# Weights and centroids laid out by channels in a clustered 1x1 convolution, and the head of its schedule reordered

## The chip, the cores and the metric

One core of one Trainium2 chip. The metric is device time in microseconds, the median of several executions. Engines are called TensorE (PE in the profile; PEld is its weight load), VectorE (DVE), ScalarE (ACT), GpSimd (POOL) and SyncE (SP), which issues the transfers.

## What is computed

The input has 8 images of 512 channels and 32 x 48 points. Each point goes to the nearest of 40 centroids by cosine; each cluster's mean over the image pulls its points, by a weight that falls with their distance; then a 1x1 convolution and a relu follow.

```python
xn = x / jnp.maximum(jnp.linalg.norm(x, axis=1, keepdims=True), EPS)
cn = centroids / jnp.maximum(jnp.linalg.norm(centroids, axis=1, keepdims=True), EPS)
sim = jnp.einsum('bchw,nc->bnhw', xn, cn)
idx = jnp.argmax(sim, axis=1)
onehot = jax.nn.one_hot(idx, N, dtype=x.dtype)
sum_x = jnp.einsum('bhwn,bchw->bnc', onehot, x)
count = jnp.sum(onehot, axis=(1, 2))
centroids_local = sum_x / jnp.maximum(count, 1.0)[..., None]
gathered = centroids_local[jnp.arange(B)[:, None, None], idx]
delta = jnp.transpose(gathered, (0, 3, 1, 2)) - x
alpha = jnp.exp(-jnp.mean(delta * delta, axis=1, keepdims=True))
y = x + alpha * delta
out = jnp.einsum('oc,bchw->bohw', W, y) + b[None, :, None, None]
return jax.nn.relu(out)
```

## The kernel before

The work is cut into 24 units of 512 points, three to an image; unit g belongs to image g // 3, and images are counted from 0 in the code (the change's words "image 2" are the second image, units 3 to 5). Channels stand on partitions in four groups (k). X[0] and X[1] hold two images, filled by turns. Every engine runs a list of instructions written out by hand, and semaphores tie them together.

Per image: `similarities(g)` multiplies centroids cT with the points; ScalarE copies the result out (`copy_sims`); `transpose_sims` turns it so that points stand on partitions; VectorE finds the first best centroid (`best_sims`, `first_best`) and writes the one-hot `oh`. `sum_clusters` multiplies it with x, for which x must have points on partitions (XT). For image 0 and for the two units in TURNED, TensorE turns x (`transpose_x`, `turn`) into the PSUM tiles gat and main, and ScalarE or VectorE evacuates it (`keep_transposed`, `keep_turned`); for the other units VectorE does it by blocks (`transpose_half`) from a blocked load XS. From the sums come the means in three bf16 parts, G (`copy_sums`, `low_clusters`, `add_halves`, `counts`, `scale_means`, `high_means`, `rest_of_mean`, `parts_of_mean`).

Per unit: `gather` brings each point its mean, `delta` on VectorE subtracts x, `square` on ScalarE and `add_chunks` on GpSimd or VectorE make squares and add channel groups, `sum_squares` on TensorE adds over partitions, `exp` on ScalarE makes alpha in the tile al, `scale` and `y_half` give y, `high_half` rounds it to its high part YH, `low_half` keeps the rest YL. Then `convolve(g, o)` multiplies in blocks of 128 output channels with three products each (WH with YH and YL, WL with YH), and `relu` evacuates. For unit 0 the first two blocks are made by `high_passes` (all products with YH), and the products with YL follow.

The weights are loaded row by row into OUT[0], each 128 x 128 block is turned on TensorE by `transpose_weights`, and `high_weights` and `low_weights` split the result into WH and WL. The centroids are loaded as rows (craw), turned on TensorE and copied to cT by ScalarE. Rows of centroids serve for the norm too. SyncE issues the centroids first, then image 0 in 12 chunks of 256 KB, the weights, the bias, image 1, and the blocked loads.

TensorE's order in the head is: warm-up products, centroids turned, similarities and transposes of image 0, weights turned (two of four groups), cluster sums of image 0, one-hot transposes, another group of weights, `add_halves(0)`, the last group, `turn(0)`, similarities of units 3 and 4, gathers of unit 0, and so on up to `convolve(0, 3)`; then the loop over units 3 to 23 begins with `gather(3, 0)`.

Of the kernel before, what the change touches and what calls it, by code (L numbers as in the profile page):

```python
# [42 lines left out]
TURNS = ((PARTS + 1, (0,)), (PARTS + 1, (1,)), (PARTS + 1, (2, 3)), (PARTS + 2, (0, 1)), (PARTS + 2, (2, 3)))  # L43
# [55 lines left out]
def build(nc, x, cent, w, bias, out):  # L99
# [3 lines left out]
    with ctx:  # L103
# [48 lines left out]
        cstat = sb("cstat", [P, 7], F32)  # L152
        Wraw = OUT[0]
# [30 lines left out]
        cT_ps, cT_done, norm_step = sem("ct_ps"), sem("ct_done"), sem("norm_step")  # L184
        wT_ps, wh_done, wl_done = sem("wt_ps"), sem("wh_done"), sem("wl_done")
# [23 lines left out]
        def wT(k):  # L209
            return (gat[:, 0, :], gat[:, 1, :], main[:, 0, :], main[:, 1, :])[k]  # L210
# [51 lines left out]
        def _(sp):  # L262
# [25 lines left out]
            sp.dma_start(craw[0:N, :], cent).then_inc(c_in, 16)  # L288
# [109 lines left out]
        def _(dve):  # L398
# [165 lines left out]
            low_weights(0)  # L564
            low_weights(1)
            low_clusters(0)
            counts(0)
            low_weights(2)
            rest_of_mean(0)
            parts_of_mean(0)  # L570
            low_weights(3)

            delta(0, 0)
            delta(0, 1)
            transpose_half(3, 0)
# [4 lines left out]
            transpose_half(3, 1)  # L580
# [12 lines left out]
            rest_of_mean(1)  # L593
            parts_of_mean(1)
            add_chunks(2, 0)
            low_half(1, 1)
# [53 lines left out]
        def _(act):  # L650
# [14 lines left out]
            def square(g, h):  # L665
                act.wait_ge(z_done, 2 * g + h + 1)
                if g < LAG:

                    act.wait_ge(wT_ps, KC)
                    act.wait_ge(const_done, 7)  # L670
                elif h == 0:
                    wait(act, s_done, folded(g - 1))
# [85 lines left out]
            def high_means(b):  # L758
# [3 lines left out]

# [3 lines left out]
            act.wait_ge(cT_ps, 1)  # L767
            a_.activation(cT[:, :, 0:N], sumP[:, 0:KC * N].rearrange("p (k n) -> p k n", k=KC),
                          ACT.Copy).then_inc(cT_done, 1)
# [9 lines left out]
            def high_weights(k):  # L779
                act.wait_ge(wT_ps, k + 1)  # L780
# [3 lines left out]
            copy_sims(1)  # L784
            keep_transposed(0, 1)
            copy_sims(2)
# [5 lines left out]
            high_weights(1)  # L792
            copy_onehot(0)
            copy_sums(0)
            evacuate_onehot()
            high_weights(2)
            scale_means(0)
            high_means(0)
            high_weights(3)
            keep_turned(0)  # L800
            act.wait_ge(b_in, 16)
            copy_sims(3)
            copy_sims(4)
# [3 lines left out]
            keep_turned(1)  # L807
            keep_turned(2)
            keep_turned(3)
            keep_turned(4)  # L810
# [5 lines left out]
            move_sums(1)  # L816
            exp(1)
            high_half(0, 1)
# [7 lines left out]
            high_half(1, 0)  # L826
            square(2, 1)
            high_half(1, 1)
# [63 lines left out]
        def _(pe):  # L892
            t_ = nc.tensor

            def similarities(g):
# [9 lines left out]
                for k in range(KC):  # L905
# [292 lines left out]
```

## Time and profile before

| | before |
|---|---|
| time, median of 3 runs | 410.26 us (409.72 to 410.3) |
| the profiled execution | 410.88 us |
| its span | 409.1 us |
| mean granted clock of TensorE | 0.999 |
| TensorE matmuls busy | 403.9 us (99%) |
| VectorE busy | 338.9 us (83%) |
| ScalarE busy | 260.7 us (64%) |
| GpSimd busy | 262.1 us (64%) |

Times inside the profile count from the start of the span; the execution's own time is 1.8 us longer than the span. Matmuls are pipelined and the durations shown overlap, so the distance between two starts says more about a matmul's cost than its duration. Busy times are of one execution.

### The profile page before, as it was taken

What the parts mean: (1) busy time and instruction counts of PE and PEld (TensorE: products, weight loads), DVE (VectorE), ACT (ScalarE), POOL (GpSimd) and SP (SyncE); (2) the same over time, 40 slices, a digit from 0 to 9 for tenths busy, and PEclk for the clock granted to TensorE, in tenths of its full rate; (3) what the DMA queues carried; (4) which work ended last, traced back from release to release, by engine and by line L of the source; (5) the groups of instructions that cost most, each with busy time, mean ns of one, the idle gap of its engine ahead of it and who ended that gap; (6) DMA issues with size and microseconds to landing.
All of it is one profiled execution on the core that took longest, in us unless ns stands there. A gap on an engine that the chain in (4) does not pass through costs nothing.

```text
span 409.1 us, 5812 instructions
## 1 busy us (share of the span) xinstructions
PE 403.9 (99%) x2088; PEld 288.2 (70%) x2088; DVE 338.9 (83%) x415; ACT 260.7 (64%) x362; POOL 262.1 (64%) x117
## 2 busy tenths in 40 slices
PE   8999999999999999999999999999999999999997
PEld 5746376775867677775867758776777758777886
DVE  2439999888899879999799898998799897898730
ACT  6566783767665684665865576656846658676641
POOL 2003773984599676994789946996769947433420
PEclk9999999999999999999999999999999999999999
DMA  7992493988499395967979575994957240222213
GB/s 256 380 248 51 88 244 84 297 252 180 172 246 266 113 281 140 272 162 183 265 198 229 191 163 188 254 256 118 276 139 226 104 129 13 103 103 104 103 68 138
DMA packets 77918, 74.51 MB, mean 182 GB/s; under 512 B 13723, under 2 KB 52891, under 8 KB 77891
## 3 DMA queue, kind: packets, MB, share of 16 engines
q1 hardware_dynamic: 77890, 74.15, 64.7%
q8 instruction: 17, 0.28, 0.3%
q14 instruction: 11, 0.08, 0.1%
HBM read 46.22 MB, written 25.17 MB: 174 GB/s over the span
## 4 chain that ended last, share of the span: by engine, by line
PE 95%; POOL 1%; DMA 1%; ACT 1%; issue 0%; DVE 0%; SPq 0%; ACTq 0%
PE main L1023 21%; PE main L1024 21%; PE main L1025 21%; PE fa L915 11%; PE sump L960 8%; PE gat L1000 5%; PE fa L924 1%; PE al L1006 1%; DMA x<-x 1%; PE main L1084 1%; PE main L1037 1%; PE al L1011 1%; POOL o L382 1%; POOL o L385 1%; PE gat L1037 1%; PE main L1055 0%
## 5 line engine op out<-in xcount | busy, mean ns | idle before, releaser
L1023 PE MATMUL main<-yh,wh 128*128 128x512 f32 (+1 forms) x376 | 152.8, 406 | 0.0
L1024 PE MATMUL main<-yl,wh 128*128 128x512 f32 (+1 forms) x376 | 146.3, 389 | 0.0
L1025 PE MATMUL main<-yh,wl 128*128 128x512 f32 (+1 forms) x376 | 146.1, 389 | 0.0
L360 POOL TENSOR_TENSOR z<-z,x 128x1024 f32<-128x1024 f32 x41 | 97.4, 2395 | 60.5 <-DVE z L519 60.5
L367 POOL TENSOR_TENSOR yl<-z,yh 128x1024 fp32r<-128x1024 f32 x43 | 103.7, 2429 | 13.8 <-ACT yh L693 13.7
L701 ACT ACTIVATE o<-main,bcol 128x512 f32<-128x512 f32 x96 | 65.1, 680 | 46.8 <-PE main L1025 45.9
L1023 PEld LDWEIGHTS main<-yh,wh 128*128 128x128 f32 x376 | 70.7, 188 | 21.4 <-issue 4.6
L1025 PEld LDWEIGHTS main<-yh,wl 128*128 128x128 f32 x376 | 70.6, 188 | 14.9
L1024 PEld LDWEIGHTS main<-yl,wh 128*128 128x128 f32 x376 | 70.7, 188 | 13.8
L374 POOL TENSOR_TENSOR xr<-xt 128x2048 f32<-128x2048 f32 x11 | 51.5, 4684 | 19.1 <-DVE xt L411 19.1
L483 DVE TENSOR_TENSOR z<-gat,x 128x1024 f32<-128x1024 f32 x46 | 55.8, 1213 | 6.1 <-PE gat L1000 6.1
L519 DVE TENSOR_TENSOR z<-z,al 128x1024 f32<-128x1024 f32 x48 | 56.3, 1210 | 0.6 <-ACT al L688 0.5
L693 ACT ACTIVATE yh<-z 128x1024 fp32r<-128x1024 f32 x48 | 50.6, 1053 | 3.6 <-POOL z L360 1.8
L915 PE MATMUL fa<-x,c_t 128*64 128x256 f32 x384 | 47.2, 394 | 0.5 <-DMA x<-x 0.5
L411 DVE STREAM_TRANSPOSE xt<-xs 128x1024 f32<-128x1024 f32 x38 | 46.1, 1225 | 0.0
L915 PEld LDWEIGHTS fa<-x,c_t 128*64 128x64 f32 x384 | 26.5, 140 | 19.3 <-issue 5.8
L673 ACT ACTIVATE sq<-z 128x1024 f32<-128x1024 f32 x21 | 22.3, 1060 | 25.7 <-DVE z L483 25.7
L673 ACT ACTIVATE gat<-z 128x1024 f32<-128x1024 f32 x21 | 21.5, 1024 | 25.2 <-DVE z L483 25.2
L419 DVE TENSOR_TENSOR xr<-xr 128x2048 bf16<-128x2048 f32 x11 | 36.7, 3338 | 0.2
L960 PE MATMUL sump<-xt,oh 128*64 128x512 f32 (+1 forms) x148 | 31.7, 537 | 0.0
L382 POOL TENSOR_TENSOR o<-o 128x512 f32<-128x512 f32 x4 | 5.1, 1284 | 36.2 <-ACT o L673 36.2
L1000 PE MATMUL gat<-oht,g 128*128 128x512 bf16 x92 | 27.8, 384 | 0.0
(139 smaller groups left out, 402.6 us busy)
## 6 DMA issues: line engine op xcount, KB each, us to landing
out<-o SPq DMA_DIRECT2D x23, 1024.0 KB, 7.2
x<-x SPq DMA_DIRECT2D x21, 1024.0 KB, 6.6
xs<-x SPq DMA_DIRECT2D x76, 256.0 KB, 5.5
x<-x SPq DMA_DIRECT2D x12, 256.0 KB, 5.4
o<-w SPq DMA_DIRECT2D x1, 1024.0 KB, 8.4
out<-o SPq DMA_DIRECT2D x3, 256.0 KB, 2.0
out<-o SPq DMA_DIRECT2D x2, 128.0 KB, 1.7
oht<-oh SPq DMA_TRANSPOSE x7, 3.7
```

The source lines that it names most:

```text
L360: pool.tensor_tensor(z, z, X[g // PARTS % 2][:, pair(h), span(g)], ALU.add).then_inc(y_pool, 1)
L367: pool.tensor_tensor(YL[g % 2][:, pair(h), :], Z[g % 2][:, pair(h), :], YH[g % 2][:, pair(h), :].bitcast(F32), ALU.subtract).then_inc(lo_p ...
L374: pool.tensor_tensor(XR[:, g % PARTS, :, :].rearrange("p t c -> p (t c)"), xt.rearrange("p t c -> p (t c)"), halfword(xt, 1), ALU.subtract ...
L483: v_.tensor_tensor(Z[g % 2][:, pair(h), :], banks(g, h)[:, :, :], X[g // PARTS % 2][:, pair(h), span(g)], ALU.subtract).then_inc(z_done, 1)
L519: v_.tensor_tensor(z, z, al[:, :].unsqueeze(1).to_broadcast([P, 2, UNIT]), ALU.mult).then_inc(za_done, 1)
L693: a_.activation(YH[g % 2][:, pair(h), :], Z[g % 2][:, pair(h), :], ACT.Copy).then_inc(hi_done, 1)
L701: a_.activation(OUT[g % 2][:, o, cols], main[:, o % 2, cols], ACT.Relu, bias=bcol[:, o:o + 1]).then_inc(relu_done, 1)
L915: last = t_.matmul(simP[u][NPAD * h:NPAD * (h + 1), :], cT[:, k, :], toks, start=(k == 0), stop=(k == KC - 1))
L960: last = t_.matmul(sumP[NPAD * h:NPAD * (h + 1), :], onehot[:, slot(u, tile), :], x_part[:, tile * C:(tile + 1) * C], start=(opens and t = ...
L1023: t_.matmul(tile, WH[:, k, rows], YH[g % 2][:, k, cols], start=(k == 0), stop=False)
L1024: t_.matmul(tile, WH[:, k, rows], YL[g % 2][:, k, cols], start=False, stop=False)
L1025: last = t_.matmul(tile, WL[:, k, rows], YH[g % 2][:, k, cols], start=False, stop=(k == KC - 1))
```

## The change

The host hands over the weights with input channels first, and a second copy of the centroids laid out by channel (partition, group, centroid). The weights go from their tile OUT[0] straight to `high_weights` and `low_weights`; the 16 transposes of weights and the four of centroids go. ScalarE's queue issues both loads of centroids, and SyncE's queue starts with image 0. The order in the head changes: similarities of unit 0 begin with k = 0 alone and four k = 0 transposes stand behind them; `transpose_sims(0)` stands ahead of unit 1's transposes; the 32 transposes of TURNED come in four steps instead of five, the first two around `add_halves(0)`. Both gathers of unit 1 stand ahead of `sum_squares_direct(0)`, and `sum_squares_direct(1)` stands behind the first half of `high_passes`. VectorE takes the halves of `transpose_half(3)` one step earlier and `low_half(1, 1)` before `parts_of_mean(1)`. ScalarE does `high_half(0, 1)` before `exp(1)`, and `high_half(1, 1)` before `square(2, 1)`.

```diff
--- before.py
+++ after.py
@@ -40,7 +40,7 @@
 TURNED = (PARTS + 1, PARTS + 2)
-TURNS = ((PARTS + 1, (0,)), (PARTS + 1, (1,)), (PARTS + 1, (2, 3)), (PARTS + 2, (0, 1)), (PARTS + 2, (2, 3)))
+TURNS = ((PARTS + 1, (0, 1)), (PARTS + 1, (2, 3)), (PARTS + 2, (0, 1)), (PARTS + 2, (2, 3)))
@@ -96,7 +96,7 @@
-def build(nc, x, cent, w, bias, out):
+def build(nc, x, cent, cent_t, w, bias, out):
@@ -181,8 +182,8 @@
         ones_done, const_done, ident_done = sem("ones_done"), sem("const_done"), sem("ident_done")
-        cT_ps, cT_done, norm_step = sem("ct_ps"), sem("ct_done"), sem("norm_step")
-        wT_ps, wh_done, wl_done = sem("wt_ps"), sem("wh_done"), sem("wl_done")
+        cT_in, cT_done, norm_step = sem("ct_in"), sem("ct_done"), sem("norm_step")
+        wh_done, wl_done = sem("wh_done"), sem("wl_done")
         xp_done, xe_dve, xe_act = sem("xp_done"), sem("xe_dve"), sem("xe_act")
@@ -207,7 +208,7 @@
         def wT(k):
-            return (gat[:, 0, :], gat[:, 1, :], main[:, 0, :], main[:, 1, :])[k]
+            return Wraw[:, k, :]
@@ -285,7 +286,6 @@
-            sp.dma_start(craw[0:N, :], cent).then_inc(c_in, 16)
             for u in range(PARTS):
@@ -561,23 +561,21 @@
             first_best(0)
-            low_weights(0)
-            low_weights(1)
+            for k in range(KC):
+                low_weights(k)
             low_clusters(0)
             counts(0)
-            low_weights(2)
             rest_of_mean(0)
             parts_of_mean(0)
-            low_weights(3)
+            transpose_half(3, 0)
             delta(0, 0)
             delta(0, 1)
-            transpose_half(3, 0)
+            transpose_half(3, 1)
             best_sims(1)
...
             delta(1, 1)
-            transpose_half(3, 1)
             scale(0, 0)
@@ -591,9 +589,9 @@
             rest_of_mean(1)
+            low_half(1, 1)
             parts_of_mean(1)
             add_chunks(2, 0)
-            low_half(1, 1)
             add_chunks(2, 1)
@@ -666,7 +664,7 @@
-                    act.wait_ge(wT_ps, KC)
+                    act.wait_ge(wl_done, KC)
                     act.wait_ge(const_done, 7)
@@ -760,13 +758,12 @@
+            act.dma_start(cT[:, :, 0:N], cent_t).then_inc(cT_in, 16)
+            act.dma_start(craw[0:N, :], cent).then_inc(c_in, 16)
...
             act.wait_ge(norm_step, 1)
-            act.wait_ge(cT_ps, 1)
-            a_.activation(cT[:, :, 0:N], sumP[:, 0:KC * N].rearrange("p (k n) -> p k n", k=KC),
-                          ACT.Copy).then_inc(cT_done, 1)
             act.wait_ge(c_in, 16)
@@ -777,45 +774,43 @@
             def high_weights(k):
-                act.wait_ge(wT_ps, k + 1)
+                act.wait_ge(w_in, 16)
                 a_.activation(WH[:, k, :], wT(k), ACT.Copy).then_inc(wh_done, 1)
...
             copy_sims(1)
+            copy_sims(2)
             keep_transposed(0, 1)
-            copy_sims(2)
             keep_transposed(1, 0)
...
             high_weights(0)
-            high_weights(1)
             copy_onehot(0)
+            for k in range(1, KC):
+                high_weights(k)
             copy_sums(0)
             evacuate_onehot()
-            high_weights(2)
             scale_means(0)
             high_means(0)
-            high_weights(3)
             keep_turned(0)
...
             copy_sims(3)
+            keep_turned(1)
             copy_sims(4)
...
             square(0, 1)
-            keep_turned(1)
             keep_turned(2)
             keep_turned(3)
-            keep_turned(4)
             exp(0)
...
             move_sums(1)
+            high_half(0, 1)
             exp(1)
-            high_half(0, 1)
             copy_sums(1)
@@ -824,8 +819,8 @@
             high_half(1, 0)
+            high_half(1, 1)
             square(2, 1)
-            high_half(1, 1)
             relu(0, 2)
@@ -892,7 +887,7 @@
-            def similarities(g):
+            def similarities(g, ks=range(KC)):
                 b, u = divmod(g, PARTS)
@@ -902,7 +897,7 @@
                 rows = X[b % 2]
-                for k in range(KC):
+                for k in ks:
                     if b == 0:
@@ -914,7 +909,8 @@
                                          start=(k == 0), stop=(k == KC - 1))
-                last.then_inc(sims_done, 1)
+                if ks[-1] == KC - 1:
+                    last.then_inc(sims_done, 1)
@@ -939,7 +935,7 @@
                 if PARTS * b + u in TURNED:
-                    pe.wait_ge(xe_act, KEPT + 3 + 2 * TURNED.index(PARTS * b + u))
+                    pe.wait_ge(xe_act, KEPT + 2 + 2 * TURNED.index(PARTS * b + u))
                 elif b > 0:
@@ -976,14 +972,9 @@
                 wait_onehot(pe, b)
-                if g == 0:
-                    pe.wait_ge(wl_done, KC // 2 * (h + 1))
-                    if h == 0:
-                        pe.wait_ge(xe_act, KEPT + 1)
-                elif g < LAG:
-                    pe.wait_ge(xe_act, KEPT + 4 + h)
+                if g < LAG:
+                    pe.wait_ge(xe_act, KEPT + 2 * g + h + 1)
                 elif h == 1:
@@ -1026,35 +1017,34 @@
-            def transpose_x(u, half):
+            def transpose_x(u, half, ks=range(KC)):
                 if (u, half) == (1, 0):
...
                     at = u * UNIT + (HALF * half + t) * P
-                    for k in range(KC):
+                    for k in ks:
                         last = t_.transpose((gat, main)[half][:, t, k * P:(k + 1) * P], X[0][:, k, at:at + P],
                                             ident[:, :])
-                last.then_inc(xp_done, 1)
-            def turn(step):
+                if ks[-1] == KC - 1:
+                    last.then_inc(xp_done, 1)
+            def turn(step, now=(0, 1)):
                 g, tiles = TURNS[step]
-                if step == 0:
-                    pe.wait_ge(wl_done, 1)
-                elif step < 3:
-                    pe.wait_ge(z_done, step)
+                if step < 2:
+                    pe.wait_ge(xe_act, KEPT - 1 + step)
                 else:
-                    pe.wait_ge(xe_act, KEPT + step - 1)
-                for i, t in enumerate(tiles):
-                    at = g % PARTS * UNIT + t * P
+                    pe.wait_ge(z_done, step - 1)
+                for i in now:
+                    at = g % PARTS * UNIT + tiles[i] * P
                     for k in range(KC):
...
                                             ident[:, :])
-                last.then_inc(xp_done, 1)
+                if now[-1] == 1:
+                    last.then_inc(xp_done, 1)
@@ -1064,19 +1054,9 @@
             pe.wait_ge(ident_done, 5)
-            pe.wait_ge(c_in, 16)
-            for k in range(KC):
-                last = t_.transpose(sumP[:, k * N:(k + 1) * N], craw[0:N, k * P:(k + 1) * P], ident[0:N, 0:N])
-            last.then_inc(cT_ps, 1)
             keep_busy(1)
-            pe.wait_ge(cT_done, 2)
-            def transpose_weights(k):
-                pe.wait_ge(w_in, 16)
-                pe.wait_ge(xe_act, 4 if k < 2 else 5)
-                for o in range(KC):
-                    last = t_.transpose(wT(k)[:, o * P:(o + 1) * P], Wraw[:, o, k * P:(k + 1) * P], ident[:, :])
-                last.then_inc(wT_ps, 1)
+            pe.wait_ge(cT_done, 1)
+            pe.wait_ge(cT_in, 16)
             def high_passes(ks):
@@ -1084,49 +1064,50 @@
-            similarities(0)
-            transpose_x(0, 0)
+            similarities(0, range(0, 1))
+            transpose_x(0, 0, range(0, 1))
+            transpose_x(0, 1, range(0, 1))
+            similarities(0, range(1, KC))
+            transpose_x(0, 0, range(1, KC))
             similarities(1)
-            transpose_x(0, 1)
             similarities(2)
+            transpose_x(0, 1, range(1, KC))
+            transpose_sims(0)
             transpose_x(1, 0)
-            transpose_sims(0)
             transpose_x(1, 1)
...
             transpose_x(2, 1)
-            transpose_weights(0)
-            transpose_weights(1)
             pe.wait_ge(const_done, 7)
...
             transpose_onehot()
-            transpose_weights(2)
-            add_halves(0)
-            transpose_weights(3)
             pe.wait_ge(x_in[1][1], 16)
             turn(0)
+            add_halves(0)
+            turn(1)
             similarities(3)
...
             similarities(5)
-            turn(1)
+            turn(2, (0,))
             transpose_sims(1)
-            turn(2)
+            turn(2, (1,))
             turn(3)
-            turn(4)
             gather(1, 0)
+            gather(1, 1)
             sum_squares_direct(0)
-            gather(1, 1)
             sum_clusters(1, 1)
...
             gather(2, 0)
-            sum_squares_direct(1)
             pe.wait_ge(z_done, 4)
+            pe.wait_ge(wl_done, KC)
             pe.wait_ge(hi_done, 1)
             high_passes(range(0, 2))
+            sum_squares_direct(1)
             pe.wait_ge(hi_done, 2)
@@ -1187,7 +1168,8 @@
         "centroids": np.ascontiguousarray(L0_conv_centroids),
-        "w": np.ascontiguousarray(L0_conv_W),
+        "cent_t": np.ascontiguousarray(np.asarray(L0_conv_centroids).T.reshape(KC, P, N).transpose(1, 0, 2)),
+        "w": np.ascontiguousarray(np.asarray(L0_conv_W).T),
         "bias": np.ascontiguousarray(L0_conv_b),
```

## Rows read from the trace of the kernel before

**Rows 1.** Busy time in a window: PE, PEld, DVE, ACT, POOL, clock, DMA.

```profile
100.00:408.00 308.00, 306.36 (x1541) 225.27 (x1539) 264.21 (x285) 195.19 (x273) 214.67 (x81) 1.00 0.61 175
```

**Rows 2.** Waits of PE, 0 to 95 us: total, times, longest.

```profile
PE al L970 <- DVE sums_l L458: 0.3, 1, 0.3
...
PE main L1037 <- ACT xt L655: 0.2, 1, 0.2
PE main L1055 <- ACT xt L662: 0.2, 1, 0.2
```

**Rows 3.** Timeline of SyncE's queue: start, duration, line.

```profile
0.74 0.43 SPq L288 DMA_DIRECT2D sq<-centroids  x1
1.22 6.06 SPq L291 DMA_DIRECT2D x<-x  x12
```

**Rows 4.** Landing of the twelve chunks of image 0 (line 291).

```profile
DMA to landing us min/median/max: 2.6/5.4/6.1
```

**Rows 5.** Landing of the 512 bias values (line 294).

```profile
DMA to landing us min/median/max: 8.1/8.1/8.1
```

**Rows 6.** Similarity matmuls, 0 to 14 us: duration min/median/max in ns.

```profile
L915 PE MATMUL fa<-x,c_t x42: 379/380/689, 4.7 to 13.9; 128*64 128x256 f32 x42
```

**Rows 7.** Timeline of PE: start, duration, line, count, idle before.

```profile
3.42 0.65 PE L1069 MATMUL sump<-ident,sq 40*128 40x40 f32 x4
...
4.72 1.12 PE L915 MATMUL fa<-x,c_t 128*64 128x256 f32 x4
6.30 2.83 PE L915 MATMUL fa<-x,c_t 128*64 128x256 f32 x12 [0.46 <-DMA x<-x]
...
19.64 1.06 PE L1077 MATMUL gat<-ident,o 128*128 128x128 f32 x8
20.63 5.37 PE L960 MATMUL sump<-xt,oh 128*64 128x512 f32 x24
25.93 0.84 PE L933 MATMUL fa<-identb,oh 128*128 128x128 bf16 x12
26.61 0.61 PE L1077 MATMUL main<-ident,o 128*128 128x128 f32 x4
...
48.01 1.10 PE L1011 MATMUL al<-o,ones 128*128 128x512 f32 x2 [0.27 <-POOL o L385]
...
55.35 0.50 PE L1023 MATMUL main<-yh,wh 128*128 128x512 f32 x1
...
60.92 0.61 PE L1000 MATMUL gat<-oht,g 128*128 128x512 bf16 x2
```

**Rows 8.** Timeline of DVE.

```profile
35.55 1.24 DVE L411 STREAM_TRANSPOSE xt<-xs 128x1024 f32<-128x1024 f32 x1
...
51.20 0.68 DVE L462 TENSOR_TENSOR sums_h<-sump,sums_h 40x512 fp32r<-40x512 f32 x1 [0.22 <-ACT sums_h L744]
...
54.45 2.73 DVE L527 TENSOR_TENSOR z<-z,x 128x1024 f32<-128x1024 f32 x1
...
59.74 0.75 DVE L476 SCALAR_TENSOR_TENSOR g<-part,cols,fa 128x512 bf16<-128x512 bf16 x1
...
61.01 1.22 DVE L534 TENSOR_TENSOR yl<-z,yh 128x1024 fp32r<-128x1024 f32 x1
```

**Rows 9.** Timeline of ACT.

```profile
37.94 1.02 ACT L662 ACTIVATE xt<-main 128x1024 f32<-128x1024 f32 x1 [0.40 <-PE main L1055]
...
49.15 0.58 ACT L688 ACTIVATE al<-al 128x512 f32<-128x512 f32 x1 [0.70 <-PE al L1011]
...
54.62 1.26 ACT L701 ACTIVATE o<-main,bcol 128x512 f32<-128x512 f32 x2
```

**Rows 10.** Timeline of POOL.

```profile
45.73 2.15 POOL L385 TENSOR_TENSOR o<-o 128x512 f32<-128x512 f32 x1
47.90 5.86 POOL L367 TENSOR_TENSOR yl<-z,yh 128x1024 fp32r<-128x1024 f32 x2
53.71 2.39 POOL L360 TENSOR_TENSOR z<-z,x 128x1024 f32<-128x1024 f32 x1
```

## The prediction

> **What bounds the kernel now.** I read the view of equal stretches first. From 100 us on TensorE is busy 306.4 of 308 us, VectorE 264, GpSimd 215, ScalarE 195 [rows 1]. So the end is set by TensorE's work plus the waits that it has in the first 61 us. Of what the edit does, only what moves TensorE's start into the steady loop (the gather of unit 3 at 60.92 [rows 7]) reaches the end, and from there it counts one for one: the loop is untouched, and the other engines are released there by TensorE's own results. The waits view and the notes in the timeline give what TensorE idles in the head: 0.46 for a chunk of image 0, 0.24 and 0.24 for evacuations of transposes, 0.29 for the low part of the cluster sums, 0.27 for GpSimd's sum of squares of unit 1 [rows 2, 7]. Everything else in the head is TensorE's own work, so taking work from it should pay, as long as VectorE, ScalarE and GpSimd keep up. Those I read in their own timelines from 49 to 62 us [rows 8 to 10]: VectorE has no idle there beyond 0.22 us, so it is the engine that can spoil the gain.
>
> **Before the first similarities (until 6.30).** Removed on TensorE: four 40x40 transposes of centroids (0.65) and the wait for their evacuation [rows 7]. They lie ahead of chunk k=1 of image 0, on which the similarities wait until 6.30, so they pay nothing by themselves. The centroid load leaves SyncE's queue: 0.43 us of issue, chunk 0 issued at 0.74 instead of 1.22 [rows 3]. Against it, two loads from ScalarE's queue share the transfer engines with the chunks: the raw centroids as before, and as many bytes again in 512 pieces of 160 B (four runs in each of 128 partitions). The gain of 0.48 on chunk 1 is an upper bound; the lower is none. I take none. ScalarE issues both loads ahead of its first table load; at 0.43 us each [rows 3] that is done by 1.7, and its first work that TensorE needs, the copies of similarities, comes after 9.1 (6.30 + 2.83 [rows 7]), behind a norm chain that loses its wait for the turned centroids. So this costs nothing.
>
> The new condition is the landing of the turned centroids. The nearest rows are chunk loads (2.6 us at least, 5.4 in the median [rows 4]) and the load of 512 single bias values behind a 1 MB load (8.1 us [rows 5]). Issued at about 0.8, it lands between 3.4 and 8.9. It is first in its own queue, as chunk 0 is second in its own today, so I take a value near the low end, 4.5. Then come the k=0 similarities and four k=0 transposes, two of each half of unit 0, which now stand in the gap before chunk 1. Every microsecond of landing beyond 4.5 costs about one.
>
> The Trainium skill (TensorE: Matmul & The Clock Gate, What's actually happening) says that the array runs at half rate until activity releases it. The durations agree with it and the granted-clock column does not. If the shorter warm-up here released it later, each microsecond of work would take two; I leave this out of the sum.
>
> **From chunk 1 to the one-hot transposes (25.93).** The four k=0 transposes no longer stand here. Eight transposes take 0.99 us from start to start (19.64 to 20.63 [rows 7]), so four are 0.5. The eight transposes of weights at 19.64 go: 0.99. The wait of 0.24 for an evacuation [rows 2] should shrink to about 0.1: turning the similarities now stands ahead of the transposes of unit 1, and the chain transpose, copy, transpose is just as long as two steps of TensorE. Nothing new is late: the one-hot on VectorE begins from an earlier turning of the similarities. The copies of weights now read the loaded tile, and ScalarE places three of them in the time of the cluster sums (5.3 us, 20.63 to 25.93 [rows 7]). Sum: 0.5 + 0.99 + 0.14 = 1.6 us earlier, at 24.3.
>
> **From there to the sum of squares of unit 1.** Today it ends 23.2 us after the one-hot transposes begin (25.93 to 48.01 + 1.10 [rows 7]). Out of that go the other eight weight transposes (0.9: 0.6 for the group of four at 26.61 with its drain, less for the second), and the waits of 0.29, 0.24 and 0.27 = 0.8, which the new order covers (whole units are turned while the cluster sums are split, and ready products stand before the sum of squares). The number of transposes for image 2 stays 32; five steps become four. In comes the first half of the high-part products of unit 0, now ahead: eight matmuls at 5.57 / 24 = 0.232 us (55.35 to 60.92 [rows 7]) = 1.9. And I expect 0.4 us of new waiting: both gathers of unit 1 need banks that ScalarE evacuates in 1.02 us each [rows 9], one behind the other, while TensorE has only the last turn to do. So 23.2 - 0.9 - 0.8 + 1.9 + 0.4 = 23.8, or 0.6 later against this start.
>
> Could TensorE do those products so early? They need the high part of y of unit 0. VectorE gets there sooner by one block transpose of 1.24 us [rows 8], which moves to where it waits for the first gather (the other stands where this one did), so it comes 1.2 sooner against the start, just before TensorE asks. GpSimd's sum of unit 1 ends at 47.88 now (45.73 + 2.15 [rows 10]), 21.95 after the start, and the products end at about 22.7. It is covered, even with 0.8 us of stretching by VectorE, as the products leave 0.75 us between the two.
>
> **From the sum of squares to the loop.** It releases the exponential (49.15), and behind that a chain without slack: scale, low clusters, scale, counts on VectorE, two steps of means and the relu on ScalarE (54.62), and only then the third block of unit 0 on TensorE, 55.35 [rows 7 to 9]. A later exponential is therefore felt. VectorE's 0.22 us of waiting at 51.20 goes, since ScalarE now does the second high half before the exponential, while it waits. Block three thus starts 0.6 - 0.2 = 0.4 later against the start, and TensorE stands still meanwhile. That is where part of the saving is given back.
>
> Then the means. The low half of unit 1 (1.22 us, 61.01) is moved ahead of the last step of the means (59.74 + 0.75 = 60.49 [rows 8]), for which unit 3's gather waits at 60.92; its slack is 0.43, so the move alone would cost 0.8 us. In its favour: the y half at 54.45 takes 2.73 us, of which about 1.5 is waiting for GpSimd, which does the other half from 53.71 to 56.10 [rows 8, 10]. GpSimd's two low halves of 5.86 us at 47.90 overlap less of VectorE's y there and may take 5. It then ends 0.5 to 1.4 us sooner against VectorE, and so does VectorE's y. Between all covered and 0.8 I take 0.
>
> **The sum.** 1.6 - 0.4 = 1.2 us. The profiled execution took 410.88 us (span 409.1); less 1.2 it is 409.7. The median of the runs shown is 0.6 below it, 410.26, so I predict 409.0 for the median. 0.2%, 0.8 us, is about what a measurement of this kernel can tell from no change.
>
> **Rivals.**
>
> *All of it pays.* Chunk 1 lands 0.4 earlier, the exponential is not later against its start, and no means are late: 0.4 + 1.6 + 0.9 of weights, 3 us, 407.3. For it: TensorE is the bound everywhere else. Against it: the chain behind the exponential, which needs about 6 us from VectorE and ScalarE. Chance 0.2.
>
> *Turned centroids or chunks late, by up to 1.2 us.* The small pieces take turns with the chunks. Landing at 5.3 instead of 4.5 leaves 0.4: 409.9. Chance 0.15.
>
> *Slower.* The same load, decisive: beyond 5.7 it takes the whole gain, at 7.0 it costs 1.3 more than that, 411.5; the bias row's 8.1 us shows that 512 small pieces behind other bytes can take this long. Against it: it has no queue ahead of it. Chance 0.12, with an array that stays at its lower rate longer.
>
> The Trainium skill (DMA: Bandwidth & Descriptors, Queues, rings and completion order) says that each transfer engine takes turns between the queues, packet by packet. No row here has two queues at work. By it, the loads from ScalarE's queue would get an even share and delay the chunks too; it speaks for these two rivals.
>
> *Unit 3's means late.* 0.8 is lost, 0.4 left: 409.9. Speaks for it: one instruction put before a step with 0.43 of slack. Chance 0.13.
>
> **Numbers.** The forecast has 0.4, with its own range from 408.4 to 409.5. Faster by over 0.2%: nearly all of it and the first rival, and a little of the others, 0.6; within 0.2%: the two that leave 0.4, part of the forecast, 0.26; slower 0.14. The range goes from 407.3 to 410.7: it takes in the first rival's value and half a microsecond of loss.
>
> **What would show it.** Cluster sums of image 0 begin near 19.0 (now 20.63); turned centroids landed by 4.5, no TensorE gap ahead of chunk 1; the one-hot transposes at 24.3; high-part products directly behind the gather of unit 2 at about 45.1; the exponential of unit 1 near 48.1; block three of unit 0 near 54.2 after a wait of over 1 us, which is new; unit 3's gather near 59.7. It would be wrong if similarities begin after 5.7, or if TensorE waits for means before unit 3's gather, or if the wait before block three isn't there.

## The result, and the profile after

The changed kernel took 411.19 us (median of 8 runs, 410.31 to 412.25) against 410.23 us before (8 runs, 409.44 to 410.59): ratio 1.0028, 95% interval 1.0017 to 1.0039. It is slower by about 1 us, where 1.2 us less was forecast (409.0) and 407.3 to 410.7 given as the range.

The profiled execution of the changed kernel is the fastest of its eight (410.31 us, span 408.5), so its span must not be set against that of before. What it shows is where the waits are. Below is TensorE's timeline (start, duration, line, tiles, count, idle before), with the loop's first gather last; it is to be read beside [rows 7], the same view of before:

```profile
5.11 0.65 PE L910 MATMUL fa<-x,c_t 128*64 128x256 f32 x4 [1.19 <-DMA c_t<-cent_t]
...
6.28 1.52 PE L910 MATMUL fa<-x,c_t 128*64 128x256 f32 x12
...
18.04 5.37 PE L956 MATMUL sump<-xt,oh 128*64 128x512 f32 x24
23.34 0.84 PE L929 MATMUL fa<-identb,oh 128*128 128x128 bf16 x12
...
46.45 1.13 PE L1002 MATMUL al<-o,ones 128*128 128x512 f32 x2
...
50.31 0.47 PE L966 MATMUL fa<-sums_h,select 128*128 128x512 f32 x1 [0.89 <-DVE sums_h L462]
...
52.97 0.59 PE L991 MATMUL gat<-oht,g 128*128 128x512 bf16 x2 [0.33 <-DVE z L483]
53.63 0.50 PE L1014 MATMUL main<-yh,wh 128*128 128x512 f32 x1
...
60.33 0.61 PE L991 MATMUL gat<-oht,g 128*128 128x512 bf16 x2 [0.96 <-DVE g L476]
```

The one-hot transposes begin at 23.34, 2.6 us sooner than before; unit 3's gather at 60.33, only 0.6 sooner. Between the two lie 36.99 us, where before had 34.99. TensorE's work fell (busy 400.1 us of 2068 matmuls, from 403.9 of 2088), and its waits rose, from 2.5 us in the view of before to 5.5 here (engine, tile and line, what it waited for; us in total, times, longest):

```profile
PE fa L910 <- DMA c_t<-cent_t: 1.2, 1, 1.2
PE al L1052 <- POOL ones L334: 1.0, 1, 1.0
PE gat L991 <- DVE g L476: 1.0, 1, 1.0
PE fa L966 <- DVE sums_h L462: 0.9, 1, 0.9
PE gat L991 <- ACT xt L660: 0.3, 1, 0.3
PE gat L991 <- DVE z L483: 0.3, 1, 0.3
PE main L991 <- ACT xt L660: 0.3, 1, 0.3
PE fa L920 <- ACT sims L710: 0.3, 1, 0.3
PE gat L1028 <- ACT xt L653: 0.2, 1, 0.2
```

The wait for the means (line 476), 0.96 us, is one of the signs that the forecast named as speaking against it. VectorE's timeline of that stretch, and below it GpSimd's:

```profile
52.73 1.75 DVE L527 TENSOR_TENSOR z<-z,x 128x1024 f32<-128x1024 f32 x1
...
57.03 2.58 DVE L534 TENSOR_TENSOR yl<-z,yh 128x1024 fp32r<-128x1024 f32 x1
59.54 0.73 DVE L476 SCALAR_TENSOR_TENSOR g<-part,cols,fa 128x512 bf16<-128x512 bf16 x1
```

```profile
40.48 3.52 POOL L382 TENSOR_TENSOR o<-o 128x512 f32<-128x512 f32 x2 [3.06 <-ACT o L671]
44.07 2.32 POOL L385 TENSOR_TENSOR o<-o 128x512 f32<-128x512 f32 x1
...
56.13 2.40 POOL L367 TENSOR_TENSOR yl<-z,yh 128x1024 fp32r<-128x1024 f32 x1 [2.73 <-ACT yh L691]
```

The low half takes 2.58 us instead of 1.22: it ends 1.08 us after GpSimd's low half of the same unit (56.13 + 2.40 = 58.53; 57.03 + 2.58 = 59.61), just as the y half of [rows 8] ended 1.08 after GpSimd's y (56.10 and 57.18). As such a VectorE instruction takes 1.22 us when it meets nothing, it did nearly all of its work behind GpSimd's end: the records overlap, but the later one waited. The same happens the other way in GpSimd's sum for unit 1. Its three additions stand from 40.48 to 46.39, 5.9 us, where before they took 4.75, from 43.13 to 47.88 ([rows 10] has the third, the first two are here):

```profile
43.13 2.53 POOL L382 TENSOR_TENSOR o<-o 128x512 f32<-128x512 f32 x2 [3.39 <-ACT o L673]
```

In the changed kernel both of VectorE's additions for y of unit 0 (line 527, at 41.60 and 44.01) lie on them, before only one did (45.46). e9 below tests this.

The Trainium skill (SBUF — State Buffer, Who interferes with whom) states this: a VectorE instruction with two SBUF inputs contends with a GpSimd instruction that reads SBUF, and the one that comes second blocks entirely. Both traces agree: 1.08 us behind GpSimd's end in each.

### The profile page after: what moved, and what is told of

It reads as the page before. It is cut to its first block, busy times and chain, and to the rows that moved or that the text cites. A ratio compares the mean times of both kernels' runs of the same rounds, so it can differ in the third digit from the quotient of the medians.

```text
span 408.5 us, 5765 instructions
## 1 busy us (share of the span) xinstructions
PE 400.1 (98%) x2068; PEld 285.4 (70%) x2068; DVE 339.0 (83%) x415; ACT 260.4 (64%) x360; POOL 262.3 (64%) x117
## 4 chain that ended last, share of the span: by engine, by line
PE 87%; SPq 5%; DVE 2%; DMA 2%; issue 2%; ACT 1%; ACTq 0%; DVEq 0%
PE main L1014 21%; PE main L1015 20%; PE main L1016 20%; PE sump L956 8%; PE fa L910 8%; PE gat L991 5%; DMA xs<-x 2%; SPq L276 2%; SPq L291 1%; PE al L997 1%; PE fa L920 1%; SPq L269 1%; PE al L1002 1%; DVE z L483 1%; ACT xt L660 0%
## 5 line engine op out<-in xcount | busy, mean ns | idle before, releaser
L367 POOL TENSOR_TENSOR yl<-z,yh 128x1024 fp32r<-128x1024 f32 x43 | 102.6, 2406 | 14.6 <-ACT yh L691 14.5
L910 PE MATMUL fa<-x,c_t 128*64 128x256 f32 x384 | 45.6, 384 | 1.2 <-DMA c_t<-cent_t 1.2
L382 POOL TENSOR_TENSOR o<-o 128x512 f32<-128x512 f32 x4 | 6.1, 1532 | 33.5 <-ACT o L671 33.5
```

What stands on the lines that cost most here:

```text
L367: pool.tensor_tensor(YL[g % 2][:, pair(h), :], Z[g % 2][:, pair(h), :], YH[g % 2][:, pair(h), :].bitcast(F32), ALU.subtract).then_inc(lo_p ...
L910: last = t_.matmul(simP[u][NPAD * h:NPAD * (h + 1), :], cT[:, k, :], toks, start=(k == 0), stop=(k == KC - 1))
```

## The experiments

All changes are to the changed kernel unless said. "One-hot at" is the start of the one-hot transposes in the run's trace, "gather" the stretch from there to the start of unit 3's gather, both in us. Times are medians of 11 or 12 executions (e1 and e17 five, e11 and e13 six, e12 seven, e5 one), and the kernel before ran beside them on the same chip, 15 to 30 times. Runs of different chips are compared by their ratios to before.

| run | time | before | ratio, 95% | one-hot at | gather |
|---|---|---|---|---|---|
| e1 again | 412.05 | 410.56 | 1.0039 (1.0026 to 1.0052) | 25.12 | 36.71 |
| e2 low half back | 410.32 | 410.56 | 0.9995 (0.9985 to 1.0004) | 23.90 | 35.75 |
| e3 more warm-up | 411.02 | 410.56 | 1.0018 (1.0009 to 1.0027) | 23.90 | 37.50 |
| e4 centroids in one piece | 411.79 | 410.56 | 1.0032 (1.0021 to 1.0043) | 23.49 | 37.24 |
| e5 before again | 411.25 (one) | 410.34 | | 26.19 | 35.01 |
| e6 before, weights alone | 409.59 | 410.34 | 0.9981 (0.9970 to 0.9992) | 24.88 | 34.78 |
| e7 low half, sum back | 410.59 | 410.34 | 1.0006 (0.9996 to 1.0016) | 24.17 | 35.56 |
| e8 low half back, k0 in order | 410.88 | 410.34 | 1.0016 (1.0004 to 1.0028) | 25.65 | 35.61 |
| e9 low half, blocks back | 410.76 | 410.69 | 1.0002 (0.9989 to 1.0015) | 23.49 | 36.25 |
| e10 low half, blocks, sum back | 410.07 | 410.69 | 0.9990 (0.9973 to 1.0007) | 23.62 | 35.57 |
| e11 as e10, warm-up | 408.96 | 410.69 | 0.9964 (0.9950 to 0.9977) | 23.22 | 35.55 |
| e12 before, low half moved | 411.92 | 410.69 | 1.0036 (1.0020 to 1.0051) | 26.24 | 36.45 |
| e13 as e11 | 409.33 | 410.57 | 0.9971 (0.9960 to 0.9982) | 23.88 | 35.59 |
| e14 as e10 | 410.57 | 410.57 | 0.9995 (0.9985 to 1.0005) | 25.28 | 35.55 |
| e15 as e3 | 411.00 | 410.57 | 1.0015 (1.0005 to 1.0025) | 23.82 | 37.18 |
| e16 as e1 | 411.57 | 410.57 | 1.0029 (1.0020 to 1.0039) | 24.80 | 36.70 |
| e17 as e11, exponential back | 408.23 | 410.32 | 0.9946 (0.9933 to 0.9960) | 23.37 | 34.65 |
| e18 low half back, warm-up | 409.94 | 410.32 | 0.9990 (0.9981 to 0.9998) | 23.47 | 36.34 |

**e1, e16: the changed kernel again.**

> The changed kernel unchanged, for a second trace and times on the same chip as the three others. The trace of it that I have shows TensorE idle in the head for about 4.3 us (1.2 for the turned centroids, 0.9 for the low sums, 0.96 for the means ahead of unit 3's gather, the rest in pieces of 0.2 to 0.3). Theory M (waits for the means and the centroids): 1.002 to 1.004 of before, and the trace again shows each of those waits. Theory C (TensorE's lower rate at the start lasts longer in the changed kernel than in before): this trace shows similarity matmuls of 630 to 690 ns until after 8 us, where the first trace of the changed kernel had them short at 5.1 us, and its span is about 1 us longer than 408.5.

> The changed kernel again: ratio 1.0025 to 1.004, spread 1.5 to 2 us.

The waits are the same, the head is not. From e1, TensorE's timeline:

```profile
4.85 1.12 PE L910 MATMUL fa<-x,c_t 128*64 128x256 f32 x4 [0.93 <-issue]
5.90 0.69 PE L1028 MATMUL gat<-ident,x 128*128 128x128 f32 x2
6.38 0.63 PE L1028 MATMUL main<-ident,x 128*128 128x128 f32 x2
6.95 2.83 PE L910 MATMUL fa<-x,c_t 128*64 128x256 f32 x12
```

The same twelve matmuls take 2.83 us here and 1.52 in the first trace (0.23 and 0.12 us from start to start), and everything behind them is later by 1.5 to 1.8 us (span 410.0 against 408.5). So both theories hold a part: M for the waits, C for a head that comes out in more than one way. e1 is to be compared with the traces of before, which have the long matmuls too: head 25.12 against 25.93, loop 61.83 against 60.92, 0.9 us later, which is about the measured loss of 1.0. Against the second trace of before (e5, below) it is 0.6.

**e2: the low half goes back.**

```diff
             rest_of_mean(1)
-            low_half(1, 1)
             parts_of_mean(1)
             add_chunks(2, 0)
+            low_half(1, 1)
             add_chunks(2, 1)
```

> Unit 1's low half goes back behind the last step of the means on VectorE, as in before. Theory M: the means for unit 3 come 2.5 us sooner, the 0.96 us wait ahead of unit 3's gather goes, no new wait comes at unit 1's convolution, and the time falls by 0.8 to 1.0 us against the changed kernel, to a ratio of about 1.000 to before. Theory C: that wait is covered by something else (GpSimd's low half or the relu), and the time falls by less than 0.3 us.

The wait is gone, as M says, the means are ready at 58.24 (57.49 + 0.75), and the low half takes 1.21 us again, since GpSimd's is over by then (58.98). GpSimd's now lies on the addition between the two, which takes 1.37 us instead of 0.68, and nothing waits for that:

```profile
57.49 0.75 DVE L476 SCALAR_TENSOR_TENSOR g<-part,cols,fa 128x512 bf16<-128x512 bf16 x1
58.16 1.37 DVE L489 TENSOR_TENSOR xr<-xr 128x512 f32<-128x512 f32 x1
59.45 1.21 DVE L534 TENSOR_TENSOR yl<-z,yh 128x1024 fp32r<-128x1024 f32 x1
```

The stretch falls from 36.99 to 35.75 (both heads are early), and the ratio, which is 1.0028 to 1.0039 for the changed kernel in three measurements, to 0.9995: 1.4 to 1.8 us, somewhat more than the 1.2 of the stretch. Unit 3's gather begins at 59.65, so the means have 1.4 us of slack in this order, where before they had 0.43 [rows 7, 8].

**e12: the same edit, alone, on the kernel before** (the diff above, backwards).

> The kernel before with one edit: unit 1's low half on VectorE ahead of the last step of the means. Theory M: it waits for ScalarE's high half (60.4) and GpSimd's low half (60.3), ends near 61.6, the means come at 62.4, and unit 3's gather waits 1.4 to 1.7 us for them; ratio 1.0035 to 1.004. My prediction's size for this edit was 0.8 us at most: ratio 1.002. Rival: taken up by slack, under 0.3 us.

The gather waits 1.3 us for the means; the stretch grows by 1.44 against e5, the kernel before traced a second time (there it is 35.01, as in the first trace), and the ratio is 1.0036. So this one line costs 1.2 to 1.5 us in either kernel. What the line meets differs. From e12, ScalarE's high half, VectorE and TensorE:

```profile
59.67 1.04 ACT L693 ACTIVATE yh<-z 128x1024 fp32r<-128x1024 f32 x1
60.75 1.23 DVE L534 TENSOR_TENSOR yl<-z,yh 128x1024 fp32r<-128x1024 f32 x1 [0.69 <-ACT yh L693]
62.69 0.60 PE L1000 MATMUL gat<-oht,g 128*128 128x512 bf16 x2 [1.26 <-DVE g L476]
```

The low half starts late, behind ScalarE, and takes 1.23, so here it is ScalarE's high half, not GpSimd (over at 60.58), that it waits for.

**e6: the weights alone, on the kernel before.** `wT(k)` is `Wraw[:, k, :]`, and the four calls of `transpose_weights` go; the waits for its banks become waits for ScalarE's evacuations.

> The kernel before with one part of the change: the weights come by channel and the 16 transposes go, all orders stay. Theory M (the part that pays, the rest costs): TensorE reaches the one-hot transposes 1.0 us sooner and unit 3's gather 1.0 to 1.4 us sooner; ratio 0.9965 to 0.9975. Rival (VectorE and ScalarE set the pace of the head, TensorE's saving turns into waits): under 0.4 us, ratio 0.999 or more.

0.8 us faster, between the two expectations. The head is 1.05 sooner than in before (24.88 against 25.93), of which 0.65 stands already at unit 1's similarities (9.47 against 10.12), where nothing of the edit has come yet. The first eight transposes save only 0.4 of their 0.99: the cluster sums now start at 19.57, as VectorE has the one-hot ready at 19.47, and TensorE stands idle for 0.49 ahead of them. Behind the one-hot transposes a new wait of 0.7 for the low sums eats most of what the other eight saved.

**e4: the turned centroids in one piece.**

```diff
-            act.dma_start(cT[:, :, 0:N], cent_t).then_inc(cT_in, 16)
+            act.dma_start(cT[:, :, :], cent_t).then_inc(cT_in, 16)
```

The host pads the array to 64 columns; the memset of the padding goes.

> The turned centroids come from the host with their zero padding, so that a partition's row is one piece of 1 KB: 128 pieces in place of 512 (and 64 columns instead of 40, half as many bytes again more). Theory of the pieces (their number makes the load land late, 4.3 us after issue): it lands 1 us or more sooner, the gap ahead of the first similarities shrinks from 1.2 us to 0.2, and if nothing else holds, unit 3's gather comes up to 0.5 us sooner; the time falls by 0.2 to 0.5 us. Theory of shared engines (it lands late because image 0 uses the engines): it still lands at about 5 us and the time stays.

It lands in 3.4 us instead of 4.3, and the first similarities start at 4.18. Nothing comes of it, neither in the time nor in the stretch: with the head early, the chunks of image 0 hold the similarities of units 1 and 2 (4.56 us for 32 matmuls that take 3.67 when nothing is awaited; 1.3 us of waits for chunks), and VectorE waits 0.45 us for the blocked load of unit 3. Pieces and bytes were changed together, so the sooner landing speaks for the number of pieces, in one trace.

**e8: no transposes ahead of chunk 1.** `similarities(0)`, `transpose_x(0, 0)`, `similarities(1)`, `transpose_x(0, 1)`, `similarities(2)`, as in before, but with `transpose_sims(0)` directly behind, as in the changed kernel.

> The changed kernel with the low half back, and the first similarities and transposes in the order of before: all four groups of unit 0's similarities, then its transposes. Theory S (four transposes at TensorE's lower rate ahead of chunk 1 delay it, from 6.3 to 6.95 in the trace with the late rate): the time falls by 0.3 to 0.6 us against the run with the low half back. Rival, my prediction's term (they fill a gap and save 0.5 us behind it): the time rises by 0.2 to 0.5 us.

Slower than e2, by 0.2% as the two ratios say; theory S fell. But the expectation's rival isn't shown either. A new wait of 0.57 for ScalarE's copy of unit 2's similarities stands ahead of `transpose_sims`, and it is all of the difference: the one-hot transposes begin at 25.65, 0.58 behind the mean of the three late heads that have the four transposes ahead (24.80 to 25.28, mean 25.07). In this trace the sixteen similarities of unit 0 follow each other from 5.00 without a pause of TensorE, so there was no gap for the transposes to fill.

**e7: the sum of squares of unit 1 back ahead of the products, too.**

```diff
             gather(2, 0)
+            sum_squares_direct(1)
             pe.wait_ge(z_done, 4)
             pe.wait_ge(wl_done, KC)
             pe.wait_ge(hi_done, 1)
             high_passes(range(0, 2))
-            sum_squares_direct(1)
```

> The changed kernel with the low half back and, besides, the sum of squares of unit 1 back ahead of the high-part products. GpSimd finishes that sum at 46.8 in the trace with the low half back, when TensorE has just done the first half of the products. Theory M: TensorE now idles about 1.9 us ahead of the sum, which it then has at the same time; the 0.9 us wait for the low sums takes part of the delay up, so the third block comes 0.7 to 1.0 us later and the time rises by that against the run with the low half back. Rival (the place of the sum is free, since the chain behind the exponential sets the third block): within 0.2 us of that run.

TensorE idles 1.9 us ahead of the sum, and the stretch is 35.56 against 35.75 in e2, which is the rival's result. The times are less clear: by the ratios this run is 0.45 us above e2, between the two expectations, with intervals that overlap, and e2's trace has an early head. By the traces the place of the sum neither gains nor loses here, as GpSimd delivers at the same time and the chain behind it sets the third block.

**e9, e10, e14: VectorE's block transposes back** (`transpose_half(3, 0)` behind `delta(0, 1)`, `transpose_half(3, 1)` behind `delta(1, 1)`); in e10 and e14 the sum of squares too.

> The changed kernel with the low half back and VectorE's two block transposes of unit 3 back in their old places, so that unit 0's y comes 1.2 us later against the one-hot transposes. Theory P (VectorE's y of unit 0, moved onto GpSimd's sum for unit 1, stretches that sum from 4.7 to 5.9 us and so holds up the sum of squares): GpSimd's three additions take 4.7 us again and end 21.9 us after the one-hot transposes, but the sum of squares stands behind the first half of the products, which now wait for y, so it comes no sooner and the time is that of the run with the low half back, within 0.4 us. Rival (the stretch comes from elsewhere): the additions stay at 5.9 us, and the time rises by 0.5 to 1.2 us.

> The same with the sum of squares of unit 1 back ahead of the high-part products, so that all of VectorE's order and this place are as in before, while the head, the turns in four steps and ScalarE's order stay changed. Theory P: the sum of squares begins 22.1 us after the one-hot transposes as in before, unit 3's gather 34.7 to 35.1 (35.6 to 35.75 with the low half alone back), and the time falls by 0.7 to 0.9 us against the run with the low half back: ratio 0.997 to 0.998, like the weights alone. Rival: ScalarE's order or the new turns hold it, and unit 3's gather stays at 35.6 or more.

> The kernel of e10 again, without the added warm-up. Both theories: ratio 0.997 to 0.999, times spread over 2 us or more; its trace shows by the first similarities whether this execution was early or late.

GpSimd's additions are short again in e9, 40.32 to 45.06, and the products wait 0.8 for y, which the expectation had. The first part of theory P stands. But in e10 the stretch is 35.57, not 35.0, and in e14 it is 35.55, with ratios of 0.9990 and 0.9995 instead of 0.997 to 0.998. ScalarE's timeline of e10 shows why.

```profile
46.48 1.06 ACT L691 ACTIVATE yh<-z 128x1024 fp32r<-128x1024 f32 x1 [0.72 <-DVE z L527]
47.57 0.58 ACT L686 ACTIVATE al<-al 128x512 f32<-128x512 f32 x1
```

The sum began at 45.34 and took 1.10; the exponential (line 686) comes at 47.57, 1.1 us later, because the second high half stands ahead of it and waits for VectorE's y.

**e3, e15, e11, e13: more warm-up.**

```diff
-            keep_busy(1)
+            keep_busy(4)
             pe.wait_ge(cT_done, 1)
```

> Three more warm-up products on TensorE stand in the gap in which it waits for the turned centroids (it idles 1.2 us there); they end before or about when the centroids land. Theory C: TensorE's rate rises earlier or more surely, and the time falls by 0.5 us or more against the changed kernel. Theory M: nothing, within 0.2 us, since the products fill idle time only.

> The changed kernel with the added warm-up, again. Theory C: 0.4 to 1.1 us under e16, ratio 1.001 to 1.002. Theory M: within 0.2 us of e16.

> The same with three more warm-up products in the gap ahead of the turned centroids. With them alone added to the changed kernel the median was 0.4 us lower, with intervals that overlap. Theory C: this one too is 0.3 us or more faster than its neighbour without them. Theory M: no difference over 0.2 us.

> The kernel of e11 again. Theory C (the warm-up makes TensorE's rate rise early in nearly every execution): again 408.7 to 409.3 us with little spread, ratio 0.996 to 0.997, and 0.6 us or more under e14. Theory M (e11 happened on lucky executions): a spread of 2 us as in e10 and a median within 0.3 us of e14.

It pays in four pairs: 0.6 us between e15 and e16 on one chip (their intervals overlap; 1.0 between e3 and e1), 1.2 between e13 and e14, 1.1 between e11 and e10. In e18 against e2, below, it is 0.2 by the ratios, within the noise. e11 runs from 408.70 to 409.02 where e10 has 408.76 to 412.14; e13 from 408.89 to 409.57. In e3, e15 and e18 the times still spread over 1.5 to 1.8 us. In all six traces with it the twelve matmuls behind chunk 1 take 1.5 us; without it five (first trace, e2, e4, e9, e10) have 1.5 and four (e1, e7, e14, e16) 2.3 to 2.8; e8, in its other order, takes 3.7 for all sixteen, the long kind too. From e13:

```profile
5.13 1.12 PE L910 MATMUL fa<-x,c_t 128*64 128x256 f32 x4
...
6.94 1.51 PE L910 MATMUL fa<-x,c_t 128*64 128x256 f32 x12
```

The Trainium skill (TensorE: Matmul & The Clock Gate, What's actually happening) says that activity releases the lower rate, and these runs agree: more matmuls ahead, and the short kind in six traces of six, against five of nine. The gain is smaller in e3 and e15 than in e11 and e13, and there is a reason: with an early head and VectorE's block transpose ahead of `delta(0, 0)`, that transpose waits for its load, 0.71 in e3 and 0.38 in e15.

**e18, e17: two combinations.**

> The changed kernel with two edits alone: unit 1's low half back, and three more warm-up products. If the two causes add up: 1.0 to 1.3 us for the low half and 0.6 for the early rate from a ratio of 1.003, so 0.998 to 0.999. If the waits for the blocked loads of image 2, which appear when TensorE is early, take the second up: 0.9995 as without it.

> The kernel of e11 and e13 with ScalarE's exponential of unit 1 back ahead of the second high half. Theory E (that order holds the exponential by 1.1 us and is the rest of the loss behind the one-hot transposes): the exponential begins within 0.1 us of its sum, unit 3's gather 34.7 to 35.1 after the one-hot transposes (35.55 without), and the time is 0.4 to 0.8 us lower: ratio 0.995 to 0.996. Rival (the new turns and gathers hold the rest): the gather stays at 35.4 or more, and the time within 0.2 us.

e18 lands at 0.9990, between adding up (0.998 to 0.999) and the other theory (0.9995), with a wait of 0.69 for the blocked load. e17 puts `exp(1)` back ahead of `high_half(0, 1)`:

```profile
46.23 0.58 ACT L686 ACTIVATE al<-al 128x512 f32<-128x512 f32 x1 [0.70 <-PE al L1002]
46.73 1.06 ACT L691 ACTIVATE yh<-z 128x1024 fp32r<-128x1024 f32 x1
```

The exponential follows its sum at once, the stretch is 34.65, and the time 408.23 us, ratio 0.9946: theory E. This version beats both kernels: before by 2.1 us, the changed one by about 3.5 (ratios 1.0028 to 1.0039). It keeps the layouts, the changed head, the four turns and the gathers' places, has the three added warm-up products, and has the old places of VectorE's block transposes and low half, of the sum of squares and of the exponential.

## Why the prediction was wrong

- **The bound, and that the head alone decides.** Right. From 100 us on the changed kernel's TensorE is busy 305.8 of 308 us.
- **"Between all covered and 0.8 I take 0"**, the low half of unit 1 ahead of the means. This is the step that failed: it costs 1.2 us in the changed kernel (e2 against the first trace) and 1.4 in before (e12). I had the blocking of VectorE by GpSimd in [rows 8, 10] and used it only in the edit's favour. That part came true: the y half shrank from 2.73 to 1.75, and the slack of the means rose from 0.43 to 1.4 us (e2), more than the 1.22 that the low half takes alone. What I didn't ask is what the moved instruction would meet at its new place, which was GpSimd's next one: it took 2.58, so the means came 2.5 us later (60.27 against 57.78 without it) and the slack was not enough. The rival "unit 3's means late" named the right wait, priced at 0.8, two thirds of it, from the instruction's own length; the blocking wasn't in it. In e12 it is 0.7 of that kind and 0.7 of waiting for ScalarE.
- **1.6 us up to the one-hot transposes.** Too much. Comparing traces with long matmuls, it is 1.05: mean of e1, e14 and e16 25.07, of before, e5 and e12 26.12. e7 is left out, as its matmuls turn short earlier (24.17; with it the gain would be 1.3). The term that is off is the landing of the centroids, taken as 4.5 with chunk 1's matmuls at 6.25; the first similarities start at 5.0 and chunk 1's at 7.0 in these traces. That the four transposes ahead of chunk 1 save 0.5 isn't shown: e8's loss is its new wait alone.
- **The rate at the start, "I leave this out of the sum".** It should have been in as a source of gain: with the gap of 0.7 to 1.3 us ahead of the centroids (first trace, e1, e2, e7 to e10, e14, e16), which the edit makes, the matmuls are short from the start of the similarities in some executions and only behind 8 us in others, and filling the gap was worth 0.6 to 1.2 us. It doesn't explain the loss. All four traces of kernels with the old head (before, e5, e6, e12) are late, but untraced executions of before seem not to be: in every trace 348.1 to 348.3 us lie between unit 3's gather and the end of the span, and the time is 1.8 longer, so the time less 350.0 gives the gather. For before, with 409.42 to 411.35 us on four chips (but for one execution of 507.06), that is an estimate of 59.4 to 61.4, where its two traces have 60.92 and 61.20. By how much the changed kernel would be behind or ahead at equal rates is not settled: no trace of before has an early head.
- **The chain from the sum of squares, 0.4 later.** Right in kind, too small in size: the third block comes 30.29 us after the one-hot transposes in the first trace and 30.0 in e1 and e16, before 29.42, so 0.6 to 0.9. GpSimd's sum was stretched from 4.75 to 5.9 us, the first half of the products covered it as I said, and by e7's trace the loss stays with or without this cover. I took VectorE's earlier y as pure gain; it is what stretches that sum (e9).
- **ScalarE's order, exponential behind the high half**, priced as a gain of 0.2. With the sum late, as in the changed kernel, it is free: the exponential follows its sum at once (46.45 + 1.13 and 47.61). With the sum on time it costs 0.9 us (35.55 in e11, 34.65 in e17). I hadn't priced the two edits against each other.

Sum of the corrected terms: 1.05 gained in the head, 1.7 lost from there to the loop (36.7 in e1 and e16 against 35.0), 0.7 later, where about 1.0 was measured; the rest is open. Of the 2.2 us between forecast and result the low half is 1.2 to 1.4. Without it (e2) the other edits gain 0.2, where 1.2 was forecast for all.

## What to carry to other kernels

When an instruction is moved in the order of VectorE, look up what GpSimd runs at its new place: here an instruction with two SBUF inputs ended 1.08 us behind GpSimd's, 2.58 or 2.73 us after its start instead of 1.22. An instruction put ahead of the last step of a chain costs what it takes there, waits included, less the chain's slack. Work taken off the engine that sets the time pays only as far as the chains that feed it move along; put each moved instruction back on its own before judging the whole. And compare heads only between executions in which TensorE's rate rises alike.

## What was unexpected of the hardware

The same kernel's first similarities run at 1.5 or 2.8 us per twelve matmuls from one execution to the next, with a granted clock of 1.00 in the records of both. With three more products of 128 x 128 in an idle gap of about a microsecond it was the shorter in six traces of six. In one kernel they cut the spread of the times from 3.4 us (e10, twelve executions) to 0.3 (e11, six) and from 1.8 (e14) to 0.7 (e13); in the changed kernel (e15, 1.8 us; e16, 1.7) they didn't. A load of 80 KB in 512 pieces took 3.8 to 4.5 us beside the chunks of image 0 (fifteen traces), and 128 KB in 128 pieces 3.4 (e4).
